# Attention's keys and queries transposed by DMA instead of TensorE, with bulk loads moved to ScalarE's queue

## The reference, cut to what matters

```python
# x [32,128,512], ctx [32,128,128]; both branches are gated and residual
x = x + tanh(g_xattn[0]) * xattn(layernorm(x), ctx, ctx)    # 32 query heads of 16, 8 kv heads, softmax over 128 keys
x = x + tanh(g_ffn[0])   * moe(layernorm(x))                # 7 routed experts, top 2, and one shared expert
# an expert: u = x @ Wup + bup;  g = silu(u @ Wgate + bgate) * u;  out = g @ Wdown + bdown   (all 512x512)
```

## Time and profile before

| | us |
|---|---|
| median of 3 runs (lowest, highest) | 1240.34 (1238.98, 1241.6) |
| the profiled execution's own time | 1239.44 |
| its span, first to last instruction | 1237.5 |
| busy in the span: PE, PEld, DVE, ACT, POOL | 1154.3, 844.5, 819.1, 534.9, 384.0 |
| mean granted TensorE clock | 0.984 |

### The profile page before, as it was taken

The page is one execution under the profiler, slowest core; times in us unless marked ns, Lnnn a source line. Parts: engine busy times, 40 slices in busy tenths (PEclk is TensorE's granted clock), DMA queues, the critical chain, the costliest instruction groups (busy, mean ns, idle before and its releaser), DMA issues.

```text
span 1237.5 us, 38404 instructions
## 1 busy us (share of the span) xinstructions
PE 1154.3 (93%) x14378; PEld 844.5 (68%) x14378; DVE 819.1 (66%) x1421; ACT 534.9 (43%) x1082; POOL 384.0 (31%) x454
## 2 busy tenths in 40 slices
PE   3868889999979999989999999999999999999997
PEld 2434444555446777778888888888888888877764
DVE  5889889999979689634444444544444444447878
ACT  2767779989889322122222222222222222222211
POOL 4465766666750000121111101111111110007762
PEclk9999899999989999999999999999999999999999
DMA  5675446565575343595744577336833364269995
GB/s 183 211 260 185 160 164 209 188 205 208 184 256 213 86 130 102 175 263 154 210 119 112 147 225 206 105 92 202 235 102 101 96 172 124 68 191 253 206 267 172
DMA packets 190496, 214.65 MB, mean 173 GB/s; under 512 B 115168, under 2 KB 115680, under 8 KB 190432
## 3 DMA queue, kind: packets, MB, share of 16 engines
q1 hardware_dynamic: 76224, 152.95, 36.7%
q10 hardware_dynamic: 103488, 25.70, 12.1%
q0 software_dynamic: 10720, 35.14, 9.6%
HBM read 324.34 MB, written 64.49 MB: 314 GB/s over the span
## 4 chain that ended last, share of the span: by engine, by line
PE 67%; DVE 13%; DMA 7%; issue 6%; POOL 3%; ACT 2%; DVEq 1%; SPq 1%; ACTq 0%; POOLq 0%
PE PS L1684 39%; PE PS L1725 19%; DVE negm L1032 5%; PE PS L1505 3%; DMA qB<-negT 2%; DMA out<-ob 2%; PE PS L1539 2%; PE PS L1525 1%; ACT x2n L861 1%; DVE xn L1018 1%; POOL whl L676 1%; DVE X L1335 1%; DVE rec L1045 1%; DVE wst L1061 1%; DMA yg<-ysl,ixf 1%
## 5 line engine op out<-in xcount | busy, mean ns | idle before, releaser
L936 ACT ACTIVATE sl<-PS,bb 128x128 f32<-128x128 f32 (+1 forms) x344 | 106.4, 387 | 428.6 <-PE PS L1684 407.1
L1684 PE MATMUL PS<-xT,wb 128*128 128x128 f16 (+1 forms) x4128 | 281.4, 230 | 4.8 <-DMA wb<-wsc 3.2
L1684 PE MATMUL PS<-uhl,wb 128*128 128x128 f16 (+1 forms) x4128 | 279.8, 229 | 1.2 <-DVE uhl L1286 1.2
L1684 PEld LDWEIGHTS PS<-uhl,wb 128*128 128x128 f16 x4128 | 265.4, 98 | 21.5 <-DVE uhl L1286 2.1
L1684 PEld LDWEIGHTS PS<-xT,wb 128*128 128x128 f16 x4128 | 265.7, 98 | 13.7 <-issue 3.4
L1725 PE MATMUL PS<-wb,ghl 128*128 128x512 f16 x1200 | 268.9, 381 | 4.5 <-DVE ghl L1298 4.5
L1725 PEld LDWEIGHTS PS<-wb,ghl 128*128 128x128 f16 x1200 | 116.2, 98 | 136.6 <-DVE ghl L1298 5.3
L926 ACT ACTIVATE u<-PS,bb 128x128 f32<-128x128 f32 (+1 forms) x344 | 106.7, 387 | 170.9 <-PE PS L1684 158.1
L1293 DVE TENSOR_TENSOR g<-sl,u 128x512 f32<-128x512 f32 x102 | 70.5, 692 | 159.3 <-ACT sl L936 156.0
L727 POOL COPY ixr<-idx 128x2 int32 (+1 forms) x35 | 6.8, 195 | 544.4 <-DMA xT<-xs 402.0
L1032 DVE TENSOR_REDUCE negm<-PS 128x8 f16<-128x1024 f32 x128 | 155.2, 1212 | 27.0 <-PE PS L1505 26.2
(11 more groups left out here) (159 smaller groups left out, 1222.2 us busy)
## 6 DMA issues: line engine op xcount, KB each, us to landing
wb<-wsc SPq DMA_DIRECT2D x219, 1024.0 KB
wst<-in_wall SPq DMA_DIRECT2D x32, 768.0 KB, 5.9
wsc<-whl SPq DMA_DIRECT2D x32, 768.0 KB, 4.3
ysl<-yb SPq DMA_DIRECT2D x43, 512.0 KB
bd<-in_bdown SPq DMA_DIRECT2D x74, 256.0 KB
X<-in_x SPq DMA_DIRECT2D x8, 1024.0 KB, 6.6
qB<-qT SPq DMA_DIRECT2D x32, 256.0 KB, 3.0
xnd<-xhl SPq DMA_DIRECT2D x32, 256.0 KB, 2.0
```

Source lines behind the costliest of these rows:

```text
L936: ins = act.activation(sl[:, m, ts], bank_of(PS[1], t, m, kind), ACT.Silu, bias=bb[:, par, bias_slot(kind, t), 1, m:m + 1], scale=1.0 / WS)
L1684: ins = pe.matmul(bank_of(bank, t, m, kind), wb[:, j, l, k, w, m * P:(m + 1) * P], rhs(x, k)[:, ts], start=(n == 0), stop=(n == len(TERMS) ...
```

## The change

The keys and queries are transposed by DMAs that SP issues (`turn_k`: 128x512, `turn_q`: 128x1024), straight from `kx` and `qx` to `kT` and `qT`; `tr_k`, `tr_q`, `evac_k` and `evac_q` are gone, and everything that waited for them waits for the DMAs' semaphores `kT_in` and `qT_in`. The two middle dimensions of `qT` and `qB` change places. In SP's body `turn_k` of b+3 stands between `load_w` and the second `neg_rows`, and `turn_q` of b+3 at the end. The constants, the later megabytes of `x` and the rest of `ctx` are issued by ACT. At the start of the routed tiles the table reads and the up-layer loads of the second tile stand ahead of the wait for the down layer, and the biases go behind.

```diff
+            def turn_k(half, par, quad):
+                b = number(half, par)
+                sp.wait_ge(S["k_split"], b + 1)
+                need(sp, S["t_done"], UNITS * (b - 3))
+                sp.nop(nofuse=True)
+                sp.dma_start_transpose(kT[:, quad, :, :, :].rearrange("p w g c -> p (w g) c"),
+                                       kx[:, par, :, :, :, :].rearrange("p w k r d -> p (w k r d)")).then_inc(kT_in[par], 16)
+            def turn_q(half, par, quad):
+                ...  # the same of qx and qT, after q_split
             def queries_again(half, par, quad):
-                if isinstance(b, int) and b < 2:
-                    sp.wait_ge(S["qT_ready"], b + 1)
-                else:
-                    sp.wait_ge(S["t_done"], UNITS * (b - 1))
+                sp.wait_ge(qT_in[par], 16 * (half + 1))
+                need(sp, S["t_done"], UNITS * (b - 1))
...
+            turn_k(0, 0, 0)
+            turn_k(0, 1, 1)
+            turn_q(0, 0, 0)
             queries_again(0, 0, 0)
+            turn_q(0, 1, 1)
             queries_again(0, 1, 1)
+            load_w(0, 0)
+            turn_k(1, 0, 2)
             neg_rows(0, 0, 0)
+            turn_q(1, 0, 2)
             neg_rows(0, 0, 1)
-            sp.dma_start(C[:, n:NB, :], ctxv[:, n:NB, :]).then_inc(c_in[1], 16)
+            load_w(1, 1)
...
                 if nx is not None:
                     neg_rows(*nx[:2], 0)
-                if isinstance(half, int) and number(half, par) + 3 < XC:
-                    load_rows([number(half, par) + 3])
                 if not start:
                     store_w(*pv, nx is None)
+                if later is not None:
+                    turn_k(*later)
                 if nx is not None:
                     neg_rows(*nx[:2], 1)
                 if after is not None:
                     queries_again(*after)
+                if later is not None:
+                    turn_q(*later)
...
             sp.wait_ge(S["l2_done"], 2 * i + 2)
             load_layer(1, e[1], 1, always)
+            e_next, c = experts(1), others(1, 1)
+            for t in range(2):
+                sp.wait_ge(S["l1_done"], 2 * i + t + 3)
+                load_layer(0, e_next[t], t, c[t])
             sp.wait_ge(S["l3_done"], 2 * i + 2)
             load_layer(2, e[1], 1, always)
             store_y(i, 1)
-            e, c = experts(1), others(1, 1)
             for t in range(2):
-                load_bias(e[t], 1, t, always)
-            for t in range(2):
-                sp.wait_ge(S["l1_done"], 2 * i + t + 3)
-                load_layer(0, e[t], t, c[t])
+                load_bias(e_next[t], 1, t, always)
...
         # ACT: load_rows(1) before high_k(0); load_rows(2) and the rest of ctx behind high_q of batches 0 and 1
                 exps(half, par, 0)
+                if isinstance(half, int) and number(half, par) + 3 < XC:
+                    load_rows(number(half, par) + 3)
...
-                if after is not None:
-                    evac_q(*after)
```

More of the change, by code:

```diff
@@ L208, in program @@
         bi_in = [[sem(f"bi_in{j}{s}") for s in range(2)] for j in range(2)]
+        qT_in = [sem(f"qT_in{j}") for j in range(2)]
+        kT_in = [sem(f"kT_in{j}") for j in range(2)]
         xT_in = [sem(f"xT_in{j}") for j in range(2)]
@@ L293, in bias_loads @@
             return {"early": 1, "routed": half - SH_A // 2 + 2 - t, "late": SLOT_TILES // 2 + 3 - par}[kind]
+        per = NB // XC
+        xv = a["x"].rearrange("b p d -> p b d")
+        ctxv = a["ctx"].rearrange("b t d -> t b d")
         def own_rows(i):
@@ L331, in load_w @@
                 sp.dma_start(wst[:, par, :, :], a["wall"][block_of(b)]).then_inc(w_in[par], 16)
[L333 to L341, removed]
@@ L361, in neg_rows @@
+            def turn_q(half, par, quad):
+                b = number(half, par)
+                sp.wait_ge(S["q_split"], b + 1)
+                sp.nop(nofuse=True)
+                need(sp, S["t_done"], UNITS * (b - 3))
+                sp.nop(nofuse=True)
+                sp.dma_start_transpose(qT[:, quad, :, :, :].rearrange("p m g c -> p (m g) c"),
+                                       qx[:, par, :, :, :, :].rearrange("p m k r d -> p (m k r d)")).then_inc(qT_in[par], 16)
             def neg_rows(half, par, pair):
@@ L392, in shared_weights @@
                     sp.wait_ge(w_out[j], 16 * KT // 2)
-                sp.wait_ge(S["tq_done"], NB)
+                for j in range(2):
+                    sp.wait_ge(kT_in[j], 16 * NB // 2)
+                for j in range(2):
+                    sp.wait_ge(qT_in[j], 16 * NB // 2)
                 sp.wait_ge(S["va_ready"], NB)
@@ L403, in body @@
                 after = follow(half, par, quad, 2)
+                later = follow(half, par, quad, 3)
                 start = isinstance(half, int) and number(half, par) == 0
@@ L946, in _ @@
                 act.wait_ge(x2_out[j], 16 * (NB // 4))
+            for j in range(2):
+                act.wait_ge(kT_in[j], 16 * NB // 2)
             turn_shared(2)
@@ L1099, in body @@
                     maxes(*nx[:2], 1)
-                if after is not None:
-                    evac_k(*after)
                 if chunk is not None:
@@ L1572, in _ @@
             scores_max(0, 0, 0, 3)
-            tr_k(1, 0)
             tr_neg(0, 0, 1)
@@ L1586, in body @@
                 scores(half, par, quad, 1, nx and (*nx, 2))
-                if after is not None:
-                    tr_q(*after[:2])
                 if not start:
@@ L1595, in body @@
                 scores(half, par, quad, 3, after and (*after, 0))
-                if later is not None:
-                    tr_k(*later[:2])
                 if nx is not None:
```

82 lines of the change are left out of this document (25 added, 57 removed).

## The result

The changed kernel takes 1264.43 us (median of 4 runs, 1253.52 to 1274.2) against 1240.97 of the kernel before beside it (4 runs, 1238.98 to 1245.52): a ratio of 1.0145, 95% interval 1.0095 to 1.0195. It is slower, where 1228 was forecast. The ratio leaves out the run of 1274.2 us, which fell in a slower state at a granted clock of 0.954 (0.963 to 0.968 in the others). Its profiled execution took 1253.52 us with a span of 1251.7, against 1237.5 before; it is the fastest of the four, so what follows accounts for 14.2 us of a loss that the ratio puts at 12 to 24.

What follows compares the result with a forecast made beforehand. DVE bounds late attention batches; early ones also wait for `neg_rows` DMAs and `split_k`; PE bounds the experts, with one gap. Terms +3.5 - 5.5 - 4.8 + 0 - 4.9 = -11.7 gave 1227.7, stated as 1228 beside the median; range 1218 to 1242.

Steps and rivals of the forecast that it cites:

- what stands ahead of `neg_rows` is an order, not a rate: Early attention batches: the argument against the rival "the loads are where they were", with moved loads no longer ahead in SP's order.
- what DMA traffic does to a landing: Attention: where the prediction said it was most likely wrong, as no row of the attention shows it.
- the loads are where they were: Rival, early batches: moved megabytes use the same engines, `neg_rows` waits as long; 1236.4 us, chance 0.19.
- The start, +3.5: Up to the first exponential: first queries land later by DMA beside bulk loads; +3.5 us, bounds +1.3 to +8.4.
- Batches 0 to 5, -5.5: Early attention: less stands ahead of `neg_rows` in SP's order; half the way to DVE's floor, -5.5 us, bounds -11 and +2.
- Batches 6 to 11, -4.8: Attention: PE no longer waits for `split_k`, DVE's copies go; -4.8 us, bounds -6.9 and -1.
- Batches 12 to 31, 0: Attention loop: removed work comes to nothing and DMA is not full; 0 us, bounds 0 and +8.
- Routed tiles, -4.9: Start of routed tiles: the 3.18 us gap and 1.7 us at half clock go; -4.9 us, bounds -3.2 and -4.9.
- The late transposes: Rival, attention: `qT` of b+3 lands late in every body, PE stands at `scores_max`; 1250 us, chance 0.17.
- DVE's gap between two maxima: Sign of right, loop: DVE's idle gap grows from 0.4 to 0.8 us, with batches of 9.2 us.
- three signs of "wrong": PE waiting for `qT` or `kT`, loop batch over 9.6 us; first exponential after 36; `neg_rows` in chain at 5 us and more.
- The bad ends: All terms at their worst bounds: +8.4 + 2 - 1 + 8 - 3.2 = +14.2 us, giving 1255 us.

Runs made afterwards that it cites:

- Experiment 6: The changed kernel with `neg_rows` of every batch but the first issued from ScalarE's queue instead of SP's: ratio 1.0362.
- 3: The changed kernel with ScalarE's second bulk issue (a megabyte of `x`, the rest of `ctx`) only after the first batch's queries have landed: ratio 1.0143.
- 9: The changed kernel with ScalarE's second bulk issue only after the second batch's queries have landed too: ratio 1.0133.
- 7: kernel 5 with the keys alone transposed by DMA and the first two loads of weights behind them: ratio 1.0105.
- kernel 5: The kernel before with bulk loads and constants on ScalarE's queue and the routed tiles' new order, all transposes on TensorE: ratio 0.9928.
- experiment 12: kernel 5 with the constants behind the second megabyte of `x` and the weights' load behind the second `neg_rows`: ratio 1.0012.
- experiment 4: The kernel before with only the bulk loads and constants moved to ScalarE's queue, transposes on TensorE: ratio 0.9962.
- experiment 14: The kernel of Experiment 13 with all bulk loads and constants back on SP, the rest of `ctx` behind the first batch's `neg_rows`: ratio 1.0068.
- Experiment 13: The changed kernel with `turn_k` as the last issue of SP's body, behind `neg_rows`, the copy to `qB` and `turn_q`: ratio 1.0145.
- experiments 2: The changed kernel with `turn_k` issued behind the second `neg_rows` of SP's body instead of ahead of it: ratio 1.0108.
- 10: The changed kernel with the next weights' load issued behind the second `neg_rows` instead of ahead of `turn_k`: ratio 1.0469.

## Why the prediction was wrong

**What failed first is a sentence, not a size:** "what stands ahead of `neg_rows` is an order, not a rate". It was used to let transfers on another queue pass. Experiment 6 shows that a small DMA on a queue of its own doesn't pass them: 5.6 us to its first packet, against 1.2 with hardly anything under way. 3, 9 and 7 show at the start that bulk on ScalarE's queue holds up what SP issues. Nor is it a strict order over all queues: in kernel 5 the first `neg_rows`, issued at 24.18 us, landed after 6.10, 3.3 us ahead of the rest of `ctx`, which ScalarE had issued at 21.47. The prediction named this as its weakest place ("what DMA traffic does to a landing"), had no row for it, and took for every term a value in the better half of its bounds all the same. The page of the Trainium skill that I had set beside the rival "the loads are where they were" says that all queues share the 16 engines, and I gave that rival 0.19.

**The start, +3.5.** It measured +10.4, beyond the upper bound of +8.4. 1.8 us is a part that the sum did not have: the first `x` lands after 7.27 us, with the constants now issued beside it, instead of 5.45 (chain of the kernel before):

```profile
0.78 5.45 DMA X<-in_x
```

In experiment 12, with the constants moved behind it, it lands after 5.7 again. The other 8.5 is the first transpose, 10.61 us from issue to landing where TensorE and ScalarE took 2.09. I took a value nearer the good end "as shares are split between queues". The DMA view of the changed kernel shows how they are split, first from 21 to 25.5 us, then from 25.5 to 26.7 (queue: packets, MB, share; q10 is ScalarE's queue, q1 SP's):

```profile
q10 hardware_dynamic: 576, 1.18, 92.3%
q1 hardware_dynamic: 532, 0.14, 14.4%
...
q1 hardware_dynamic: 524, 0.13, 50.5%
q10 hardware_dynamic: 56, 0.08, 24.0%
```

In the 4.5 us before, from the issue at 16.49 to 21, q1 moved nothing. Then about one small packet (256 B) goes for each large one (2 KB) while the bulk lasts, and when it is through, the other half follow in 1.2 us. The shares are split by packets, not by bytes, and the transpose lands with the end of the bulk: about the bad end that the prediction had worked out, plus the 1.8.

**Batches 0 to 5, -5.5.** They measured +2.6. The moved loads alone are worth what was said (-5.4 in experiment 4, -6.5 in 5, over the six batches), in part by luck: the reason given was that `neg_rows` would leave the chain, and it still stands there three times in both. The transposes of the same batches, at a DMA share of 0.91 instead of 0.78 in kernel 5, take it back: 8.81 us for one of them in batch 1, and `neg_rows` still in the chain at 4.7 to 5.2 us. Here the sum had a floor of busy time and half the way to it; the transposes' traffic was in the floor but not in the landing of what came behind them.

**Batches 6 to 11, -4.8.** They measured -0.4. That PE stands no more for `split_k` was right, and in experiment 14 these batches take 3.9 us less, the removed copies included; in the changed kernel `neg_rows` is late instead: three pieces of it, 4.7 to 4.9 us, in the chain between 107 and 178 us, behind the weights and the keys.

**Batches 12 to 31, 0.** This step failed by where I looked. I worked out whether the transposes are in time, and they are: the queries land in 2.7, 3.5 and 4.9 us (min, median, max) between 190 and 345 us, within the 5.1 that I allowed. Of `turn_k` ahead of the second `neg_rows` I asked only whether its wait for `split_k` holds SP; it doesn't. What I didn't ask is what its transfer does to the DMA behind it, which PE wants 2.5 to 2.9 us after its issue: 14.0 us of waiting instead of 0.4, and +8.1 us in all, the upper bound. Experiment 13 shows that this term could have been 0, with another order (179.7 us against 179.5).

**Routed tiles, -4.9.** Right. Tile 30 is reached 397.0 us after the first one-hot matmul instead of 402.0, and there is no gap and no half clock at the place of the earlier trace rows:

```profile
572.00:576.00 4.00, 4.00 (x76) 4.00 (x74) 1.81 (x3) 0.00 (x0) 0.00 (x0) 1.00 1.03 211
```

Of the 15 kernels with the new order eight reach tile 30 at 397.0 (the changed one among them), five between 397.6 and 399.6, and two at 405.0 and 405.6, by other gaps. The further 4.3 us in the row of the table are the last tiles: from tile 30 to the end the same code took 321 to 341 us in these executions, so they say nothing of the change. The 2.7 us of the row above it lie in such a spread as well: kernels 4 and 5, alike there, differ by 2.4 us from batch 31 to the first up layer.

**The rivals.** The late transposes were the nearest in total (1250), but with another transfer late than the one named; as named they came in experiments 2 and 10. Of the signs given, DVE's gap between two maxima did grow to 0.74 us, as said, and cost nothing by itself (in experiment 13 the loop is at 9.23 without the copies, too); of the three signs of "wrong" two were there (a first exponential after 36, `neg_rows` at about 5 us in the chain), and the third by half: a batch took 9.60 us, but PE waited for `qB`, not for `qT` or `kT`.

**The sum of bounds.** The bad ends added up to +14.2, and the profiled execution is 14.2 us longer in its span. That these are equal is chance: the attention's terms came to +20.7 where their bad ends were +17.4, and the two other rows to -6.6 where the bad end was -3.2. It is no chance that they failed together. I had let the range end at 1242, as if the terms failed independently; in the main they had one cause, a transfer on the path behind large ones.

## What to carry to other kernels

Before work is given to DMA, find the small transfers on the path and list what will have been issued ahead of each of them, by any queue; a transfer that is in time itself can still be what makes the next one late. If a stream of DMAs is added, try it last in the body, behind every transfer that something waits for: here that alone decided between 9.23 and 9.60 us a batch in the loop. It is no cure where more traffic comes on top: in the early batches the keys themselves were then late, and over the whole time the gain could not be told (experiment 13). And terms of a sum that share a resource share their bad ends.

## What was not expected of the hardware

- A 4 KB DMA on an otherwise idle queue started 5.6 us after its issue, when 1.5 MB that another queue had issued around it was through; with hardly anything under way it started after 1.2 us (experiment 6).
- Eight 128x128 blocks transposed by DMA landed in 3.0 to 3.2 us with no bulk beside them, and in 10.6 and 13.9 us beside it (experiments 9 and 3, and the changed kernel). The 1309 ns a block of the Trainium skill, "VectorE: DVE Perf Modes", "The three transpose paths", would be an estimated 10.5 us for the eight, one after another; here the eight overlap when alone. The rule of that page of the Trainium skill ("Rules for kernel authors") to take TensorE where PSUM will do agrees with these runs all the same: no kernel with a transpose of keys or queries by DMA came below the kernel before (ratios 1.0068 to 1.0469).
- DMA engines 0.86 busy over the loop cost it nothing, once the order was right (experiment 13).
